# Attention layer on one core: half of the value product taken as high and low parts, with the transposed probabilities moved by query tile

## The reference, cut to what matters

```
xn   = layernorm(x)
q, k, v = split(xn @ w_qkv.T)            # 16 heads of 128
q, k = rope(q), rope(k)
attn = softmax(q @ k.T / sqrt(128))      # 1024 x 1024 for each head and sequence
out  = (attn @ v) @ w_out.T
ffn  = gelu(xn @ mxfp4(up) + b1) @ mxfp4(down) + b2
y    = x + out + ffn
```

## Time and profile before

| | |
|---|---|
| median of 3 runs | 2508.67 us (2503.35 to 2509.61) |
| profiled execution | 2508.02 us, span 2506.2 us |
| PE busy | 2457.5 us, 98% |
| PE weight loads | 2139.8 us, 85% |
| DVE busy | 1982.2 us, 79% |
| ACT busy | 1437.6 us, 57% |
| POOL busy | 1392.9 us, 56% |
| DMA packets | 267289, 396.28 MB, queue share 59.9% |

### The profile page before, as it was taken

One profiled execution on the slowest core, in us unless ns is written; L12 is line 12 of the kernel. 1 busy time (PEld: TensorE's weight loads), 2 busy tenths in 40 slices (PEclk: granted clock), 3 DMA queues, 4 the chain that ended last, 5 costly groups with the idle time before them and its releaser, 6 DMA issues. The chain is left out here.

```text
span 2506.2 us, 41398 instructions
## 1 busy us (share of the span) xinstructions
PE 2457.5 (98%) x12656; PEld 2139.8 (85%) x12656; DVE 1982.2 (79%) x3204; ACT 1437.6 (57%) x2648; POOL 1392.9 (56%) x1115
## 2 busy tenths in 40 slices
PE   6999999999999999999999999999999999999899
PEld 4888888888888888888888888888888888888688
DVE  6877878787887878788787878878787887878576
ACT  5656666565656566565656556655555566565233
POOL 6567656665655555565556555655555565555031
PEclk9999999999999999999999999999999999999999
DMA  4665666656665555656665655656575565655842
GB/s 135 167 168 151 173 159 161 172 157 189 179 163 147 151 153 153 157 146 188 173 164 143 160 150 151 159 146 185 152 183 146 151 159 152 158 140 144 231 141 68
DMA packets 267289, 396.28 MB, mean 158 GB/s; under 512 B 38496, under 2 KB 120800, under 8 KB 267104
## 3 DMA queue, kind: packets, MB, share of 16 engines
q1 hardware_dynamic: 267232, 395.67, 59.9%
HBM read 91.43 MB, written 35.65 MB: 51 GB/s over the span
## 5 line engine op out<-in xcount | busy, mean ns | idle before, releaser
L1020 PE MATMUL o_ps<-keys_first,v_rows 128*128 128x256 f32 x4096 | 930.9, 381 | 10.4 <-DMA keys_first<-turned_blocks 10.4
L1020 PEld LDWEIGHTS o_ps<-keys_first,v_rows 128*128 128x128 f32 x4096 | 767.7, 191 | 110.4 <-DMA keys_first<-turned_blocks 11.6
L1020 PE MATMUL s_ps<-seq_parts 128*128 128x512 f32 x3072 | 834.3, 409 | 12.7 <-ACT probs L689 8.0
L792 DVE TENSOR_REDUCE neg_max<-s_ps 128x1 f32<-128x1024 f32 x512 | 611.3, 1203 | 160.3 <-PE s_ps L1020 160.1
L689 ACT ACTIVATE probs<-s_ps,neg_max 128x1024 f32<-128x1024 f32 x512 | 568.7, 1111 | 247.9 <-DVE neg_max L792 241.7
L1020 PEld LDWEIGHTS s_ps<-seq_parts 128*128 128x128 f32 x3072 | 577.9, 189 | 133.6 <-ACT probs L689 12.1
L804 DVE STREAM_TRANSPOSE turned_blocks<-probs 128x512 f32<-128x512 f32 x1024 | 662.9, 685 | 32.2 <-ACT probs L689 10.3
L558 POOL TENSOR_TENSOR rope_a<-rope_a,cos 128x512 f32<-128x512 f32 x250 | 324.6, 1298 | 633.1 <-ACT rope_b L673 633.1
L563 POOL TENSOR_TENSOR seq_parts<-rope_a,seq_parts 128x512 fp32r<-128x512 f32 x250 | 320.5, 1282 | 288.4 <-ACT seq_parts L680 288.4
L1020 PE MATMUL slot_ps<-seq_parts,w_parts 128*128 128x512 f32 x1506 | 386.9, 392 | 4.8 <-DMA seq_parts<-xnt_parts 4.8
L680 ACT ACTIVATE seq_parts<-rope_a 128x512 fp32r<-128x512 f32 x250 | 157.6, 630 | 387.9 <-POOL rope_a L561 386.4
(11 more groups left out here) (111 smaller groups left out, 1733.6 us busy)
## 6 DMA issues: line engine op xcount, KB each, us to landing
keys_first<-turned_blocks SPq DMA_DIRECT2D x2048, 128.0 KB, 2.7
w_parts<-w_qkv_parts SPq DMA_DIRECT2D x72, 512.0 KB, 4.3
seq_parts<-xnt_parts SPq DMA_DIRECT2D x14, 1024.0 KB, 8.3
w_qkv_parts<-w_parts SPq DMA_DIRECT2D x24, 512.0 KB, 3.7
wo_parts<-w_out_parts SPq DMA_DIRECT2D x48, 256.0 KB, 3.1
w_raw<-in_w_qkv SPq DMA_DIRECT2D x24, 256.0 KB, 4.3
y<-in_x SPq DMA_DIRECT2D x16, 256.0 KB, 3.3
ln_x<-in_x SPq DMA_DIRECT2D x16, 256.0 KB, 3.4
```

Source lines behind the costliest of these rows:

```text
L792: nc.vector.tensor_reduce(neg_max[:, k2 % 16:k2 % 16 + 1], s_ps[k2 % 2][:, :], AXX, ALU.max, negate=True).then_inc(max_ready, 1)
L1020: ins = nc.tensor.matmul(out, w, m, start=(n == 0), stop=(n == len(terms) - 1))
```

## The change

The first four of the eight key tiles (`SPLIT = 4`) of the value product are now taken in three float32r passes; the last four stay float32. For that v of those tiles is held as `v_hi` (copied by ACT) and `v_lo` (subtracted by DVE from PSUM, `v_low`), and the probabilities as `p_hi` (copied by ACT from `keys_first`, `probs_high`, 1024 elements per partition and chunk) with the low part written back over `keys_first`. POOL subtracts the first two tiles (`FRONT`, 512 elements) of every chunk, and the next two (`BACK`, 512 elements) of chunks 1, 2, 3 and 6 of a pair; DVE takes `BACK` of chunks 0, 4, 5 and 7.

- `move_tile` takes the place of `move_chunk`: 4 DMAs for each query tile, 128 KB each, in runs of 1 KB and no longer 2 KB. Keys of a tile are now set by their remainder by 4, so the key half of q/k is stored in that order (`by_remainder`), which makes some reads of rope's sum strided.
- `turn` is one transposition of 1024 elements per tile where it was two of 512. Tile 0 of the next chunk is turned at the end of a step, tile 1 at its start.
- Each engine's step is written in another order. On POOL `probs_low` of the chunk before stands first in every step and rope is cut into `rotated_sum` and `rotated_low`. On ACT `probs_high` stands last in every step.
- Layernorm's mean and final scaling go from DVE to ACT. `quantise` has 13 parts at other places.
- The first group of a pair's q and k is projected one half step earlier ((3, 0) becomes (2, 1)); v groups come in the tile order 1, 2, 0, 3.

The diff, cut to its core:

```diff
-        v_rows = sb("v_rows", [P, 2, BT, 2 * HEAD])
+        v_rows = sb("v_rows", [P, 2, BT - SPLIT, 2 * HEAD])
+        v_hi = sb("v_hi", [P, 2, SPLIT, 2 * HEAD], F32R)
...
-            def move_chunk(c, n, first):
+            def move_tile(c, k, t):
-                slot = n % 2
-                sp.wait_ge(blocks_turned, c * 2 + 2)
-                if not (first and n < 2):
+                slot = k % 2
+                sp.wait_ge(blocks_turned, c * 2 + t + 1)
+                if t == 0 and c >= 2:
                     sp.wait_ge(o_ready, c - 1)
                 for a in range(QUADS):
-                    for half in range(2):
-                        sp.dma_start(keys_first[half * (P // 2):(half + 1) * (P // 2), slot, a]...
+                    sp.dma_start(keys_first[:, slot, t * QUADS + a].rearrange("p j q -> p (j q)").bitcast(F32),
+                                 turned_blocks[a * QUAD:(a + 1) * QUAD, slot, t].rearrange("p b j q -> p b (j q)")
+                                 ).then_inc(keys_moved[k % 4], 16)
...
+            def probs_low(c, k):
+                slot = k % 2
+                pool.wait_ge(p_hi_ready, c + 1)
+                low = keys_first[:, slot, :, FRONT, :]
+                nc.gpsimd.tensor_tensor(low, low.bitcast(F32), p_hi[:, slot, :, FRONT, :].bitcast(F32),
+                                        ALU.subtract).then_inc(p_lo_front, 1)
+                if k % 8 in BACK_BY_POOL:
+                    ...
+                if not (first and k == 0):
+                    probs_low(c - 1, k - 1)
...
+                if k8 == 5 and more_pairs:
+                    rotated_low(p + 1, "qk0", 1)
+                    rotated_sum(p + 1, "qk0", 2)
+                if k8 == 6 and more_pairs:
+                    rotated_low(p + 1, "qk0", 2)
+                    rotated_sum(p + 1, "qk0", 3)
+                    rotated_low(p + 1, "qk0", 3)
...
+                    if k % 8 == 5 and more_pairs:
+                        rotated_high(p + 1, "qk0", 2)
+                    probs_high(i, k)
...
+            def v_low(p, parity, n, bank):
+                at = 2 * V_TILES[n]
+                dve.wait_ge(v_ready, p * 4 + n + 1)
+                nc.vector.tensor_tensor(v_lo[:, parity, at:at + 2, :], bank.rearrange("p (a b) -> p a b", a=2),
+                                        v_hi[:, parity, at:at + 2, :].bitcast(F32), ALU.subtract).then_inc(v_lo_ready, 1)
...
+                pe.wait_ge(p_hi_ready, c + 1)
+                for kt in range(SPLIT):
+                    nc.tensor.matmul(out, v_hi[:, parity, kt, cols], p_hi[:, slot, :, kt, :], start=(kt == 0), stop=False)
+                    nc.tensor.matmul(out, v_lo[:, parity, kt, cols], p_hi[:, slot, :, kt, :], start=False, stop=False)
+                pe.wait_ge(p_lo_front, c + 1)
...
+                for kt in range(SPLIT):
+                    nc.tensor.matmul(out, v_hi[:, parity, kt, cols], keys_first[:, slot, :, kt, :], start=False, stop=False)
...
+                for kt in range(SPLIT, BT):
+                    last = nc.tensor.matmul(out, v_rows[:, parity, kt - SPLIT, cols], keys_first[:, slot, :, kt, :].bitcast(F32),
+                                            start=False, stop=(kt == BT - 1))
```

More of the change, by code:

```diff
@@ L45 @@
 MX_HALF = MX_COLS // 2
+SPLIT = 4
 def layer(nc, d):
@@ L240, in group_at @@
                 return None
-            ahead = k // 8 + (1 if k % 8 >= 3 else 0)
+            ahead = k // 8 + (1 if k % 8 >= 2 else 0)
             if last and ahead > 1:
@@ L479, in batch @@
                                      d["mx"][:, MX_COLS - MX_STEP:]).then_inc(mx_w_loaded[1], 16)
+                    if not (last and n == SEQ_CHUNKS - 1):
+                        move_tile(b * SEQ_CHUNKS + n + 1, n + 1, 0)
+            move_tile(0, 0, 0)
             batch(0, True, False)
@@ L539, in rotate @@
             eng.wait_ge(own, before * 4 + 2)
-            engine.tensor_tensor(hi, a, b, ALU.add).then_inc(own, 1)
+            engine.tensor_tensor(hi, a_in, b_in, ALU.add).then_inc(own, 1)
             eng.wait_ge(own, before * 4 + 3)
@@ L613, in step @@
                     wo_low(p + 1, 0)
-                if k == 2:
-                    guess(i + 2, LN_COLS)
-                for slot in (0, 1):
-                    g = group_at(k, slot, last)
-                    if g and g[1] != "v":
-                        p = i * 2 + g[3]
-                        rotate_rest(p, g[1], g[2])
             steps_splitting(pool, step)
@@ L726, in step @@
                 more = splitting and not (isinstance(p, int) and p + 1 >= PAIRS_PER_SEQ)
+                more_pairs = not (last and k >= 8)
                 tail = last and k >= 16
@@ L938, in _ @@
             row_max(1, 1)
+            for (place, part, n), bank in zip(FIRST_GROUPS, FIRST_BANKS):
+                if part == "v" and n in V_SPLIT:
+                    v_low(0, 0, n, bank)
+            turn(0, 0, 0, True)
             def step(i, k, first, last):
@@ L945, in step @@
                 if not tail:
-                    turn(i, k, 0, first)
+                    turn(i, k, 1, first)
                 if has_out:
                     low_out(c - 2, k % 2)
-                if not tail:
-                    turn(i, k, 1, first)
+                if (k - 1) % 8 in BACK_BY_DVE and not (first and k == 0) and not (last and k == 17):
+                    probs_low(c - 1, k - 1)
+                g = None if tail or (first and k == 0) else group_at(k - 1, 1, last)
+                if g and g[1] == "v" and g[2] in V_SPLIT:
+                    v_low(i * 2 + g[3], g[3] % 2, g[2], slot_ps[:, 1])
                 if (k - 1, 1) == LN_SLOT:
@@ L960, in step @@
                     row_max(t + 3, 2 * k + 3)
+                g = None if tail else group_at(k, 0, last)
+                if g and g[1] == "v" and g[2] in V_SPLIT:
+                    v_low(i * 2 + g[3], g[3] % 2, g[2], slot_ps[:, 0])
                 if has_out:
@@ L963, in step @@
                     add_out(c - 2, (k - 2) % 16, (i // 4) if k >= 2 else ((i - 1) // 4))
-                if k == 0:
-                    dve.wait_ge(ln_loaded, (i + 1) * 16)
-                    mean(i + 2, ln_x, LN_COLS)
-                if k == 3:
+                if not tail and not (last and k == 15):
+                    turn(i, k + 1, 0, first)
+                if k == 4:
                     newton(i + 2, LN_COLS)
-                if k == 4:
-                    normalise(i + 2, ln_x, ln_xn, LN_COLS)
+                if first and k == 0:
+                    quantise(i, 0)
+                    quantise(i, 1)
                 for part in MX_PARTS.get(k, ()):
-                    quantise(i, part)
+                    if k < 15:
+                        quantise(i, part)
+                    elif not last:
+                        quantise(i + 1, part)
             steps(dve, step)
```

236 lines of the change are left out of this document (172 added, 64 removed).

## The result

The changed kernel takes 2590.31 us (median of 4 runs, 2586.74 to 2591.81); beside it on the same chip the kernel before takes 2508.09. The ratio is 1.0329, 95% interval 1.0311 to 1.0347: 3.3% slower, where 2470 was forecast and 2426 to 2511 was the range. The profiled execution has a span of 2584.9 us against 2506.2, at a mean clock of 0.994.

A forecast was written before the change was run, and what follows sets the result against it. PE's own work (98% busy) was taken to bound the kernel: 2508.0 - 77 (matmuls) + 31 (wait before step 7) + 6 (other steps) + 2 (start-up, `quantise`) = 2470 us, own range 2450 to 2488, overall 2426 to 2511.

The forecast's parts named there:

- matmuls: PE's value product: 8 passes go, 12 of 256 columns come; 3.17 us, 0.30 less per chunk, 77 us over 256 chunks.
- the wait at steps 7 and 15: PE's scores at the start of step 7 wait for POOL's low part, 0.9 to 1.0 us per pair, 31 us.
- steps 1, 2, 9, 10: Waits of PE around a pair's start: between 0 and 0.8 us per pair, taken as 0.2, 6 us in all.
- start-up and `quantise`: Start of the kernel and the other moved parts of `quantise`: 2 us added.
- the one from step 7 to step 2: Rest of the pair: slack at steps 7 and 0, about none in 1 and 2; 0.2 us per pair, 6 us.
- The chain of steps 2 to 7: In-order waits through moves, ACT, POOL and DVE end at 44.0 us; PE arrives at 43.1, so waits 0.9 to 1.0.
- the fourth low part: POOL's last q/k low part in step 6 (`qk_ready`), awaited by step 7's scores; forecast to end at 44.0 us.
- The moves land later: Rival, chance 0.05: moves in 1 KB runs land after 4.3 us, first link grows 1.6, 51 us in all, 2521.
- POOL becomes the bound: Rival, chance 0.11: seven strided POOL instructions per pair; from 1.45 us each no faster, 2519 at 1.5, 2557 at 1.67.
- More is late: Rival, chance 0.22: DVE meets POOL in all four subtracting steps; 0.6 to 1.3 us more per pair, 2489 to 2511.
- DVE beside POOL: DVE's two-operand subtraction waits for POOL's running instruction, priced in step 5; without it 0.5 us less per pair, 15 us.

The follow-up runs named there:

- e9: The changed kernel with PE's program of the 16 rounds written out, no loop on PE: 2586.98 us, ratio 1.0312 to the kernel before.
- e6: The changed kernel with DVE's low parts of the probabilities left out (output differs): 2503.91 us, ratio 0.9991 to the kernel before.
- e1: The changed kernel with keys in plain order, no remainder order in their sums and copies (output differs): 2571.28 us, ratio 1.0264 to the kernel before.
- e11: The changed kernel with two split tiles instead of four and no back low parts on DVE or POOL: 2478.09 us, ratio 0.9893 to the kernel before.
- the early sum: The changed kernel with POOL's products and sum of the fourth q/k group moved from step 6 to the end of step 5: 2542.10 us, ratio 1.0153.

## Why the prediction was wrong

By its own terms, in us (waits from the table of steps, times 16):

| term | forecast | measured |
|---|---|---|
| matmuls | -77 | -67 |
| the wait at steps 7 and 15 | 31 | 54 |
| steps 1, 2, 9, 10 | 6 | 75 |
| step 3 | 0 | 8 |
| loop branch, step 4 | not seen | 22, in the shadow (e9) |
| start-up and `quantise` | 2 | 11 |
| old waits that go, and the edges of the averages | 0 | -24 |
| sum | -38 | +79 |

**The matmuls** were priced well: 3.20 against 3.17 for the product, 0.264 against 0.30 a step.

**The step that failed is the one from step 7 to step 2**: "slack at steps 7 and 0 and about none in steps 1 and 2 ... I take 0.2". It was the one part of the pair that was not worked through instruction by instruction. It was given 0.2 us per pair and took 2.3, and 69 of the 117 us of error lie there. Two things were missed. The v group was moved to the last place of the pair, (1, 0), and its copy now stands behind the exponential; the new product waits for it after its twelve short passes. And DVE's low part was put with its price into step 5 only, though it stands in front of the row maxima in steps 0, 1, 5 and 6 of each pair (after chunks 7, 0, 4 and 5). For steps 1 and 2 the prediction names it ("DVE's subtraction delays ACT") and gives it no price; in step 1 it was the link that was late. e6 shows the waits of steps 1, 9 and 2 gone with the low part. That of step 10, 26 of the 75 us, is not settled by it: 5.6 us are the wait for layernorm's tokens, which stood in step 11 before, and for the rest e6 shows only that step 10 stays long.

**The chain of steps 2 to 7** had the right form and the right wait at its end, but every link was too short. From the end of chunk 0's product, forecast and median over 21 pairs: high part of chunk 2 8.4 and 8.9; chunk 3 16.6 and 18.3; chunk 4 26.1 and 28.4; chunk 5 35.6 and 37.8; the fourth low part 44.0 and 46.8. 1.7 of the 2.8 us are there by chunk 3, after a step 2 in which PE itself was 1.2 late (the high part of chunk 3 waits for moves that wait for PE's product). The strided copies, put at nothing, are a smaller part: with keys in plain order (e1) chunk 4's high part came at 27.6 and not at 28.4, and the fourth low part no sooner. Since PE reached step 7 at 46.0 and not at 43.1, the wait grew less than the chain did. These medians mix two kinds of pairs: before step 7 the low part ends at 47.5 and PE arrives at 46.4, before step 15 it ends at 46.0 and PE arrives at 44.4. The chain of the first kind holds step 4 with the long branch.

**The rivals.** "The moves land later" is false: the moves of 1 KB runs land after 2.7 us, as before:

```profile
keys_first<-turned_blocks SPq DMA_DIRECT2D x2048, 128.0 KB, 2.7
```

The 2 KiB that the Trainium skill gives in "DMA: Bandwidth & Descriptors", section "Why a DMA increments its semaphore by 16 and not by 1", did not matter here, between SBUF and SBUF. "POOL becomes the bound" had the right side, and its price of 1.45 us an instruction was passed by the keys' low part (1.56) but not by the six others:

```profile
L604 POOL TENSOR_TENSOR keys_first<-keys_first,seq_parts 128x512 fp32r<-128x512 f32 x256 | 336.4, 1314 | 353.8 <-ACT seq_parts L770 353.3
```

Its 353 us of waiting in that line show that POOL was not full either. "More is late" named the true mechanism, DVE meeting POOL more often; it stopped at 1.3 us per pair more, where the waits of steps 7, 15, 1, 2, 9 and 10 alone are 4 us per pair (129 us) and 37 of them were forecast.

**DVE beside POOL.** The meeting was in the sum once a pair. This line of the changed kernel says how often it happens, duration min/median/max:

```profile
L945 DVE TENSOR_TENSOR keys_first<-keys_first,seq_parts x128: 669/1319/1989, 58.2 to 2454.1; 128x512 fp32r<-128x512 f32 x128
```

With POOL at 76%, double the lone price is the middle case and three times the worst. The Trainium skill, "GPSIMD Engine Reference", Specifications, says that POOL and VectorE share SBUF interfaces; the trace agrees. The prediction had only DVE pay for it. POOL pays too: its rope low parts (L597) take 1568 ns on the mean, and 1415 in e6.

**What stays open.** How much of the 86 us in e6 is DVE's own time and how much is POOL's slowing by it was not separated, and neither was the share of the dear branch in what e11 gained. Two things were not traced: the 11 us of the start beyond the one wait of 7.0 us for the low part of chunk 0, and the greater part of step 10's wait.

## What to carry to other kernels

When work moves from the full engine to three that are less full, walk every step of the cycle in each engine's order, not just the one that looks tightest: here 69 of 117 us of error lay in the steps that were waved through. Of a change whose side costs sit on in-order chains, try the half dose first: two split tiles gave 1.1%, four lost 3.3%, since here half the dose brought half the gain and almost none of the waits. And of a wait that is found, take it away in a run before it is counted: the dear branch was real and worth 3 us at most here, the early sum looked small and was worth 48.

## What the hardware showed that was not expected

- PE's loop branch takes 0.2 us with 774 matmuls in the body and 3.6 us with 806; nine packets of 16 KB of instructions are then fetched in each round. 1.3 us of it reach PE's work.
- Float32 elements four apart: ACT's copy of 512 goes from 0.63 to 1.14 us, POOL's subtraction from 1.28 to 1.56, a float32r matmul of 512 moving columns from 0.23 to 0.45.
- The meeting of DVE and POOL slows both: POOL's subtraction of 512 elements fell by 0.15 us on the mean when DVE's low parts went, and single ones took 2.0 us. A DVE operation on eight elements took 0.17 us with POOL idle and 1.06 beside it, ending 26 to 30 ns behind POOL's instruction in all 16 cases.
